# Two partial tables instead of four for the accumulating scatter of a graph layer's edge sums

## What is computed

```
s, v   = x[:, :64] @ W_nl0, x[:, 64:] @ W_nl1          # per node
w      = relu(edge_feature @ W_fc1) @ W_fc2            # per edge, 224 weights
xs, xv = s[dst], v[dst]                                # dst is sorted
tp     = concat(w0*xs, w3*(xv.sh1), (w1*xs)*sh1, w2*xv, w4*cross(xv, sh1))
agg    = segment_sum(tp, src, num_segments=3125) / 32  # src is in no order
out    = agg @ W_out + skip
x      = layernorm(x + gate(out))                      # silu on 64, sigmoid gate on the rest
```

## Time and profile before

| what | value |
|---|---|
| median of 3 runs | 2825.72 us |
| the profiled execution | 2825.36 us |
| its span | 2823.5 us |
| PE busy | 2604.4 us (92%) |
| POOL busy | 2071.6 us (73%) |
| DVE busy | 1632.9 us (58%) |
| ACT busy | 887.5 us (31%) |
| scatters of L681 | 784, 1218.0 us busy, mean 1554 ns |
| first and last scatter start | 1288.0 us and 2748.7 us |

### The profile page before, as it was taken

One profiled execution on the slowest core, in us unless ns is written; L12 is line 12 of the kernel. 1 busy time (PEld: TensorE's weight loads), 2 busy tenths in 40 slices (PEclk: granted clock), 3 DMA queues, 4 the chain that ended last, 5 costly groups with the idle time before them and its releaser, 6 DMA issues. The chain is left out here.

```text
span 2823.5 us, 80757 instructions
## 1 busy us (share of the span) xinstructions
PE 2604.4 (92%) x24172; PEld 2231.0 (79%) x24172; DVE 1632.9 (58%) x4318; ACT 887.5 (31%) x1988; POOL 2071.6 (73%) x1825
## 2 busy tenths in 40 slices
PE   4799999999999998979999999999999999999970
PEld 2477777777777777868999999999999999999960
DVE  5365555555555555515666666666666666666646
ACT  1111111111111112124444444444444444444430
POOL 3477777777777775236888888888888888888881
PEclk9999899898889888559999999999999999999985
DMA  4333333333333333247888878888888888878765
GB/s 129 106 110 102 107 100 105 101 106 101 101 103 106 102 101 81 99 159 134 143 143 143 142 143 143 143 143 143 143 143 144 143 144 141 145 142 144 141 98 168
DMA packets 388993, 355.58 MB, mean 126 GB/s; under 512 B 60992, under 2 KB 340928, under 8 KB 388416
## 3 DMA queue, kind: packets, MB, share of 16 engines
q0 software_dynamic: 150528, 141.40, 33.4%
q1 hardware_dynamic: 228256, 204.77, 25.7%
q10 hardware_dynamic: 10176, 9.03, 1.1%
HBM read 244.75 MB, written 135.90 MB: 135 GB/s over the span
## 5 line engine op out<-in xcount | busy, mean ns | idle before, releaser
L681 POOL DMA_INDIRECT tab<-summed,sidx x784 | 1218.0, 1554 | 272.2 <-issue 208.9
L634 POOL DMA_INDIRECT gat<-f,gidx x784 | 764.8, 976 | 247.8 <-issue 228.6
L1147 DVE TENSOR_TENSOR prod<-ps_w,xg 128x768 f32<-128x768 f32 x392 | 375.3, 958 | 281.5 <-issue 169.7
L937 PE MATMUL ps_o<-ro_v,prod 128*128 128x96 f32 x3136 | 478.2, 275 | 0.0
L937 PEld LDWEIGHTS ps_o<-ro_v,prod 128*128 128x128 f32 x3136 | 413.2, 192 | 0.0
L927 PE MATMUL ps_w<-hid,wf 64*128 64x128 f32 x4704 | 368.7, 289 | 1.2 <-DVE prod L1147 1.2
L773 ACT ACTIVATE xg<-ps_x 128x768 f32<-128x768 f32 x392 | 296.3, 808 | 199.5 <-PE ps_x L959 193.9
L927 PEld LDWEIGHTS ps_w<-hid,wf 64*128 64x128 f32 x4704 | 293.5, 187 | 69.4 <-issue 44.6
L946 PE MATMUL ps_d<-msg,same 128*128 128x193 f32 x1568 | 332.4, 334 | 1.3 <-ACT summed L792 1.3
L935 PE MATMUL ps_o<-ro_s,prod 96*128 96x96 f32 x1568 | 329.9, 292 | 0.6 <-DVE msg L1158 0.6
L1016 DVE TENSOR_TENSOR ta<-ps_w,gat 128x512 f32<-128x512 f32 x196 | 135.5, 691 | 295.4 <-DMA gat<-f,gidx 237.4
(11 more groups left out here) (183 smaller groups left out, 3354.8 us busy)
## 6 DMA issues: line engine op xcount, KB each, us to landing
src_bc<-in_src_rows SPq DMA_DIRECT2D x196, 256.0 KB
tabw<-feat SPq DMA_DIRECT2D x784, 36.0 KB
ea<-in_ea SPq DMA_DIRECT2D x196, 128.0 KB
feat<-fst SPq DMA_DIRECT2D x25, 576.0 KB, 2.8
gat<-f,gidx POOLq DMA_INDIRECT x784
hot_dst<-in_dst_rows SPq DMA_DIRECT2D x98, 128.0 KB
hot_dir<-sh_rows SPq DMA_DIRECT2D x98, 128.0 KB
dst_bc<-hot_dst SPq DMA_DIRECT2D x196, 64.0 KB
```

Of the source, the lines that this page charges most:

```text
L634: pool.indirect_dma_start(out=gat[:, r % 4, k, :], out_offset=None, in_=t["f0"], in_offset=bass.IndirectOffsetOnAxis(ap=gidx[:, r // 4, at ...
L681: pool.indirect_dma_start(out=t["tabs"][into[k]], out_offset=bass.IndirectOffsetOnAxis(ap=sidx[:, r, k:k + 1], axis=0), in_=summed[:, r, k ...
L937: last = pe.matmul(ps_o[:, k, 96 + 64 * c:192 + 64 * c], prod[:, ur % 2, k, 1 + c, :], ro_v[:, c, :], start=True, stop=True)
L1147: dve.tensor_tensor(prod[:, r % 2, :, :, :].rearrange("p k c e -> p k (c e)"), ps_w4[:, :, 0:3 * P], xg[:, r // 2, r % 2 * 2:r % 2 * 2 + 2 ...
```

## The change

There are two tables. Tile k of each pair (k = 0 or 1) adds to table k, so each scatter waits for the one two tiles ahead of it, which is the same tile of the pair before. The wait for `sidx_done` comes first, and each of the two scatters has its own wait for its own table directly ahead of it. ACT's wait for a slot of `summed` means the same two scatters as before, in the numbering of the new semaphores. Its loop starts four pairs later, since more pairs are written out ahead of it. In the closing stage SP and ACT load one table each, DVE adds the two into `so`, and POOL has nothing to do. Where the tables are zeroed, SP issues half as many DMAs.

```diff
-NTAB = 4
+NTAB = 2
...
                 def scatter(u, j, r):
-                    into = [(r * 2 + k) % NTAB for k in range(2)]
+                    since(pool, sidx_done, u + 1)
                     for k in range(2):
-                        since(pool, tab_in[into[k]], 16 * (j * 2 + r // 2))
-                    settled(pool, sidx_done, u + 1, passed)
-                    for k in range(2):
+                        settled(pool, tab_in[k], 16 * u, passed)
                         pool.indirect_dma_start(
-                            out=t["tabs"][into[k]],
+                            out=t["tabs"][k],
                             out_offset=bass.IndirectOffsetOnAxis(ap=sidx[:, r, k:k + 1], axis=0),
                             in_=summed[:, r, k, 0:OW], in_offset=None, compute_op=ALU.add,
-                        ).then_inc(tab_in[into[k]], 16)
+                        ).then_inc(tab_in[k], 16)
...
                         for k in range(2):
-                            since(act, tab_in[(ur * 2 + k) % NTAB], 16 * (uj * 2 + ur // 2 - 1))
+                            since(act, tab_in[k], 16 * (u - 3))
                         act.activation(summed[:, ur, :, :], ps_d[:, :, 0:LW], ACT.Copy).then_inc(sum_done, 1)
                 gathered(0, 0)
-                split_steps(act, NPAIR, 2, step, 4, short=2)
+                split_steps(act, NPAIR, 3, step, 4, short=2)
...
             tabs = sb(c5, "tabs", [P, NC, NTAB, FT, OW])
-            tsum = sb(c5, "tsum", [P, 2, 2, FT, OW])
...
                 for m in range(NC):
-                    for k in range(2):
-                        sp.dma_start(tabs[:, m, k, :, :], tile_rows(t["tabs"][k], m)).then_inc(tin[m], 16)
+                    sp.dma_start(tabs[:, m, 0, :, :], tile_rows(t["tabs"][0], m)).then_inc(tin[m], 16)
...
-            @block.gpsimd
-            def _(pool):
-                for m in range(NC):
-                    pool.wait_ge(tin[m], 16 * NTAB)
-                    since(pool, so_done, m - 1)
-                    pool.tensor_tensor(tsum[:, m % 2, 1, :, :], tabs[:, m, 2, :, :], tabs[:, m, 3, :, :],
-                                       ALU.add).then_inc(half2_done, 1)
-
             @block.scalar
             def _(act):
                 for m in range(NC):
-                    for k in range(2, NTAB):
-                        act.dma_start(tabs[:, m, k, :, :], tile_rows(t["tabs"][k], m)).then_inc(tin[m], 16)
+                    act.dma_start(tabs[:, m, 1, :, :], tile_rows(t["tabs"][1], m)).then_inc(tin[m], 16)
...
                     dve.wait_ge(tin[m], 16 * NTAB)
-                    dve.tensor_tensor(tsum[:, r, 0, :, :], tabs[:, m, 0, :, :], tabs[:, m, 1, :, :], ALU.add).then_inc(half_done, 1)
-                    dve.wait_ge(half_done, m + 1)
-                    dve.wait_ge(half2_done, m + 1)
-                    dve.tensor_tensor(so[:, r, :, :], tsum[:, r, 0, :, :], tsum[:, r, 1, :, :], ALU.add).then_inc(so_done, 1)
+                    dve.tensor_tensor(so[:, r, :, :], tabs[:, m, 0, :, :], tabs[:, m, 1, :, :], ALU.add).then_inc(so_done, 1)
```

More of the change, by code:

```diff
@@ L1265, in gnn_kernel @@
             tin = [sem(c5, f"tin{i}") for i in range(NC)]
-            half_done, half2_done, so_done, sg_done, upd_done, res_done, bs5, mv5 = (
-                sem(c5, n) for n in ("half_done", "half2_done", "so_done", "sg_done", "upd_done", "res_done", "bs5", "mv5"))
+            so_done, sg_done, upd_done, res_done, bs5, mv5 = (
+                sem(c5, n) for n in ("so_done", "sg_done", "upd_done", "res_done", "bs5", "mv5"))
             lv5, lr5, on_done, ch5, o_out = sem(c5, "lv5"), sem(c5, "lr5"), sem(c5, "on_done"), sem(c5, "ch5"), sem(c5, "o_out")
```

## The result

| kernel | median (lowest to highest), us | runs | profiled, us | span, us | granted clock |
|---|---|---|---|---|---|
| before | 2826.73 (2823.81 to 2832.56) | 4 | 2825.36 | 2823.5 | 0.92 |
| changed | 3224.01 (3220.74 to 3228.29) | 4 | 3223.82 | 3222.0 | 0.92 |

The changed kernel takes 1.1408 times as long, with a 95% interval of 1.1389 to 1.1428: 397 us more. 3270 had been forecast, within 3035 to 3520, with the middle case at 3150 to 3390.

What follows compares the result with a forecast made beforehand. POOL's scatter issue and PE were taken as level in bounding the edge stage. The median 2825.7 us plus 462 for the scatter's wait, 0 for zeroing and ACT's loop, minus 18 in the closing stage gave 3270 us, range 3035 to 3520.

Steps and rivals of the forecast that it cites:

- the middle case: Whole kernel: the forecast of 4.9 us a pair, give or take 0.3, so 3150 to 3390 us; 46%.
- What bounds the kernel: Edge stage: POOL's scatter issue at 1.85 us and PE without a gap are level; table waits cost next to nothing.
- L: Edge stage: time from a scatter's start on POOL to its landing, taken as 4.1 us.
- w: Edge stage: time from a landing to the start of the scatter that waited for it, taken as 0.8 us.
- The pair, 4.9 us: Edge stage: two scatters take L + w = 4.9 us instead of 3.72, +462 us over 392 pairs.
- Part 2: First-layer zeroing with 196 fewer DMAs, and ACT's loop with more written out ahead: costed at 0.
- Part 3: Closing stage: first update 12.8 us earlier by fewer loads, 5.7 us from fewer additions, in sum -18 us.
- The same in both: Closing stage: 6.36 us from the last scatter's start to the first load, before and after the change.
- The clock: Edge stage: PE's idling lowers its clock, time expected to stand; rival, if not covered, 3510 us, 15%.
- The rival of a covered wait: Edge stage: L + w up to 3.72 us, POOL never waits, only the 18 us gain remains: 2808 us; 5%.
- The heavy load: Edge stage: loads fall on each scatter waited for, a pair takes 5.58 us: 3537 us; 13%.
- What the prediction said would show it: Edge stage and end: POOL idle about 0.9 us a scatter, PE three quarters busy, stage about 1920 us, DMA share about 0.6.

Runs made afterwards that it cites:

- e2: Kernel before with a separate wait ahead of each of a pair's scatters, still reaching four tiles back: 2820.77 us, ratio 1.000.
- e3: Changed kernel with POOL's scatter loop written out, so a wait can stand on the DMA itself: 3140.21 us, ratio 1.114.
- e5: e3 with the wait for a pair's first table put ahead of the one for sidx: 3097.85 us, ratio 1.098.
- e1: Kernel before, four tables and its own closing stage, but each scatter waits for the one two tiles ahead: 3224.42 us, ratio 1.143.
- e4: Kernel before with the changed kernel's closing stage, tables 2 and 3 left out of the result: 2799.73 us, ratio 0.993.
- e8: Changed kernel with three tables, each scatter waiting three tiles back, waits in the loop: 2834.12 us, ratio 1.003 to the kernel before.
- e6: Changed kernel with the stage's loads other than the broadcast source numbers made for the first two groups alone: 3202.21 us, ratio 1.134.
- e7: Changed kernel with the 256 KB broadcast source load made twice, the second into an unread tile: 3513.16 us, ratio 1.244.
- e9: Changed kernel with 16-bit source numbers, half the bytes, on a third chip: 3624.79 us, ratio 1.113 to the kernel before there.
- e11: e8 with POOL's loop written out and the table's wait on the DMA, on a third chip: 3224.03 us, ratio 0.991 to the kernel before there.

## Why the prediction came out right, step by step

- **What bounds the kernel.** "Either one, slowed down, sets the end": POOL was slowed by 1.05 us a pair, and the whole of it stands in the time. e2 showed that the old wait was free.
- **L, taken as 4.1 us.** Close, and in part by luck. The upper anchor, 4.29 us, was read as a landing without load. By the landing records that scatter (2733.88) took 4.18 us, and of the eight after it seven took 3.43 to 3.55 and one 4.18. Beside the two slow ones a packet of 16 KB of the queue that part 3 of the page calls "instruction" starts, 2.15 and 1.60 us after them; that it held them up is not shown. Without load L is thus about 3.5 us, so 4.1 stands 0.6 above it, and the loads added 0.44 at the tile that counts. L is also not one number: the pair's second tile sets the pace (some 95% of the second tiles waited), the first tile has slack to give up. Mean L of the second tiles is (3.60 + 4.29) / 2 = 3.94 us, and 3.94 + 0.79 = 4.73, against 4.78 measured. The other 0.05 is pairs in which the first tile was the later one. In the eight kernels whose scatter waits for the one two tiles ahead, the greater of the two tiles' mean L + w is 0.02 to 0.12 us below T, and 0.23 in e7.
- **w, taken as 0.8 us** from a row whose 0.82 was also POOL's pace: 0.79 measured. The other row, 0.28, was no outlier; it is what a wait on the DMA's own instruction costs (0.27 in e3 and e5), and the ground for telling the two apart was their form.
- **The pair, 4.9 us.** It took 4.78. The term is +411.5 us instead of +462; the miss of 46 us in the total is this one: L at the binding tile was 0.16 us less than taken.
- **Part 2 at nothing.** The first scatter starts 3.4 us later, and in e1, e3 and e5, with four or two tables, 4 to 6 us earlier than before. Nothing to be seen.
- **Part 3, -18 us.** -19.3: the first update comes 23.63 - 10.35 = 13.3 us earlier after the first load (12.8 worked out), and the later additions give 6.0 (5.7). e4 has the same 19.4 without the rest of the change.
- **"The same in both": the 6.36 us from the last scatter to the first load.** Wrong by 2.8 us. The trace's records hold a drain on POOL at the end of the stage, 2.4 us before, 5.3 us after and 3.5 us with three tables (e8). It goes with the tables and not with the wait: 9.2 to 9.4 us in all kernels with two, 7.5 with three, 6.35 to 6.47 with four (e1 among them, where the last landings were waited for just as closely). What the drain does in it is open.
- **The clock.** "I expect the clock to fall and the time to stand" and "its granted clock below 1.00" fell: 0.99, with five dips of 3.4 to 6.8 us in 1825, although PE idles 315 us in 382 pairs, in turn some 0.35 to 0.65 and 1.05 to 1.24 us at a time. In e6 and e7 the clock did fall, to 0.91, and the time was set by POOL all the same (L + w gives 4.64 and 5.28 us of 4.75 and 5.51). The first-layer rows from which the rival was made, idles of 0.68 and 0.91 us, don't carry over to this stage.
- **The rival of a covered wait.** It would have had L + w at 3.72 us or less. The smallest mean of L of any group of scatters is 3.52 us (e6), and 3.5 to 3.6 us is usual where hardly another load is in flight: with the loop's w that is at least 4.3 us, over 3.72 by 0.6, and even with a w of 0.27 it would be 3.8. The 2.2 us that the Trainium skill's page "DMA: Bandwidth & Descriptors", section "Anatomy of one DMA — SWDGE (gpsimd) path", gives by its fit are not seen; counted from the end of POOL's 1.54 us, not from its start, they would give an estimate of 3.7 us after its start, near the 3.5.
- **The heavy load.** 5.58 us a pair is what e7 came to (5.51) with one load more. The price was sized right, its case was not this kernel's.
- **What the prediction said would show it.** POOL's idle time 0.85 us (about 0.9 said), ACT's copies put down to the tables 386 of 392 times, PE busy 83% (three quarters), first to last scatter 1872 us (1920), DMA share 0.66 (0.6), last scatter to the end 58.4 us (57).

Not tried: two tables with the scatters waiting four tiles back as before. There nothing would keep two additions to the same row apart, so what the wait is worth against no wait at all is left open.

## What to carry to other kernels

Where an operation waits for the last one of its kind on the same target, the time from one to the next is the landing time plus the start after the landing, divided by how many operations back the wait reaches; read both from rows of the loaded stage, for the operation of the cycle that is waited for, and not as a mean. Here two targets were one too few, three just enough with the wait on the DMA itself, and four made the form of the wait free. A sum of additions saved at the end (19 us) is small beside a wait in a loop of 392 turns, each microsecond of which is 392.

## What the runs showed of the hardware

- An accumulating indirect DMA of 128 rows of 768 bytes keeps POOL for 1.54 us, can follow another every 1.85 us, and lands some 3.5 us after its start when no load is in flight (the medians of the last eight scatters of the stage are 3.48 to 3.55 us in ten kernels), 3.6 to 5.0 beside loads (means).
- From a landing to the start of the waiting DMA it takes POOL 0.27 us if the wait stands on the DMA's instruction, and 0.75 to 0.79 if it is one of its own ahead of it. Where two waits stood ahead of the DMA, only the later one stood on it, so their order was worth 42 us from e3 to e5.
- Beside the 256 KB load that spreads one row over all 128 partitions, a scatter lands 0.6 to 1.2 us later, and with half the bytes hardly less (4.28 to 4.15 us). Taking the other loads away, 400 KB a group, gave 22 us in all; the broadcast load then fell on another scatter. Where it falls in the cycle decides what it costs, and taking other loads away moves it.
- L isn't independent of the pace: when e3 took 0.5 us out of w, L of the second tile rose by 0.26.
- PE's granted clock stayed at 0.99 through 1825 us with idles of some 0.5 and 1.1 us in turn, and was 0.91 in e6 and e7. I have no row that says why.
- On one chip the first layer, whose DMA work is gathers, took 400 us longer for every kernel, at a mean granted clock of 0.67 in the middle of it, while the second layer's pace was the same to 0.01 us (e9 and the changed kernel: 4.79 and 4.78). The two rows, the kernel before on its chip and e11 on that one:

```profile
200.00:1000.00 800.00, 766.52 (x5647) 607.08 (x5645) 434.94 (x1250) 124.92 (x354) 609.83 (x625) 0.89 0.37 103
```

```profile
400.00:1400.00 1000.00, 907.86 (x4976) 708.30 (x4976) 385.88 (x1109) 107.54 (x313) 549.81 (x556) 0.67 0.27 72
```

POOL made 625 gathers in 800 us on the one and 556 in 1000 on the other.
